# Four of 32 product-key blocks computed from gathered rows instead of dense products, in a two-layer kernel on one core

## The reference

```python
s, i = jax.lax.top_k(sim, k)                       # per head: 8 of 64 keys in either half
all_scores = (sx[..., :, None] + sy[..., None, :]).reshape(b, n, h, k * k)
scores, pk = jax.lax.top_k(all_scores, k)          # 8 of the 64 pairs
idx = jnp.take_along_axis(all_idx, pk, axis=-1)    # 8 heads x 8 = 64 of 4096 rows per token
w_down, w_up = key_in[idx], key_out[idx]
o = jnp.einsum('bnd,bnhkd->bnhk', inputs, w_down)
o = gelu(o) * softmax(scores)
out = jnp.einsum('bnhk,bnhkd->bnd', o, w_up)
```

## Time and profile before

| | |
|---|---|
| median of three runs | 2982.59 us |
| profiled execution, first to last instruction (its span) | 2977.3 us |
| what the three runs have around such a span | about 5.3 us |
| TensorE busy with matmuls | 2840.2 us, 95% of the span |
| VectorE busy | 1919.1 us, 64% |
| ScalarE busy | 1215.2 us, 41% |
| GpSimd busy | 491.4 us, 17% |
| mean granted TensorE clock | 0.985 |
| product-key and LSTM stage, from the first L1008 to the last L1077 | 425.8 to about 1971 us |

### The profile page before, as it was taken

How to read it: one execution, slowest core, us unless ns; L and a number is a source line. 1 busy time by engine, 2 the same in 40 slices (tenths; PEclk the granted TensorE clock), 3 DMA queues, 4 the chain that set the end, 5 groups by cost and what they waited for, 6 DMA issues and landing times.

```text
span 2977.3 us, 72660 instructions
## 1 busy us (share of the span) xinstructions
PE 2840.2 (95%) x28558; PEld 2187.9 (73%) x28558; DVE 1919.1 (64%) x6577; ACT 1215.2 (41%) x2721; POOL 491.4 (17%) x616
## 2 busy tenths in 40 slices
PE   8999979999999999999999999978999859999998
PEld 4895467777777777777777777645676639999998
DVE  4553587777777777777777777466777654444443
ACT  2332232333334343434343333235555525555554
POOL 0555400000000000000000000012334313333333
PEclk9999989999999999999999999999999979999999
DMA  3552300101010000101010101111222232222222
GB/s 141 175 158 82 140 2 23 33 23 34 23 34 30 26 32 25 36 24 34 23 34 23 33 23 33 37 36 41 70 77 63 59 121 33 37 37 40 37 37 33
DMA packets 94322, 148.90 MB, mean 50 GB/s; under 512 B 20048, under 2 KB 76240, under 8 KB 90896
## 3 DMA queue, kind: packets, MB, share of 16 engines
q1 hardware_dynamic: 73728, 107.83, 11.0%
q0 software_dynamic: 20112, 36.40, 6.0%
q10 hardware_dynamic: 144, 0.03, 0.0%
HBM read 95.93 MB, written 48.27 MB: 48 GB/s over the span
## 4 chain that ended last, share of the span: by engine, by line
PE 87%; DVE 6%; DMA 2%; ACT 2%; issue 2%; SPq 0%; POOL 0%; POOLq 0%; DVEq 0%; ACTq 0%
PE ps L1008 16%; PE ps L827 15%; PE ps L2075 9%; PE ps L1077 8%; PE ps L2090 8%; PE ps L1044 4%; PE ps L989 4%; PE ps L420 2%; PE ps L431 2%; PE ps L857 2%; PE ps L858 2%; PE ps L1560 2%; PE ps L1516 1%; PE ps L266 1%; PE ps L267 1%
## 5 line engine op out<-in xcount | busy, mean ns | idle before, releaser
L827 PEld LDWEIGHTS ps<-arena 128*128 128x128 f32 x4096 | 536.4, 192 | 29.1 <-issue 2.9
L1008 PE MATMUL ps<-arena 128*128 128x256 f32 x2048 | 550.7, 392 | 3.0 <-DVE arena L998 2.0
L827 PE MATMUL ps<-arena 128*128 128x128 f32 x4096 | 538.9, 276 | 0.9 <-ACT arena L835 0.9
L1008 PEld LDWEIGHTS ps<-arena 128*128 128x128 f32 x2048 | 354.7, 190 | 164.1 <-issue 132.9
L835 ACT ACTIVATE arena<-ps 128x256 f32<-128x256 f32 x512 | 196.0, 383 | 546.4 <-PE ps L827 545.9
L1077 PE MATMUL ps<-arena 128*16 128x256 f32 x4096 | 270.6, 382 | 8.4 <-DVE arena L1107 7.6
L2075 PE MATMUL ps<-arena 128*128 128x128 f32 x2272 | 265.4, 275 | 0.1
L1803 POOL MEMSET arena<- 128x3072 f32 x1 | 2.7, 2658 | 1569.6 <-PE ps L1008 1569.6
L2075 PEld LDWEIGHTS ps<-arena 128*128 128x128 f32 x2272 | 259.4, 192 | 0.4 <-issue 0.3
L2090 PE MATMUL ps<-arena 128*128 128x256 f32 x1136 | 256.8, 379 | 0.0
L1098 DVE SCALAR_TENSOR_TENSOR arena<-arena 128x128 f32<-128x128 f32 x256 | 73.7, 288 | 280.6 <-ACT arena L1089 280.6
(11 more groups left out here) (287 smaller groups left out, 4631.3 us busy)
## 6 DMA issues: line engine op xcount, KB each, us to landing
xw_scratch<-arena SPq DMA_DIRECT2D x32, 512.0 KB, 2.7
arena<-xw_scratch SPq DMA_DIRECT2D x256, 64.0 KB, 2.7
arena<-in_W SPq DMA_DIRECT2D x16, 1024.0 KB, 5.2
ys_scratch<-arena SPq DMA_DIRECT2D x71, 128.0 KB, 1.8
xn_scratch<-arena SPq DMA_DIRECT2D x32, 129.0 KB, 3.0
arena<-in_xT SPq DMA_DIRECT2D x8, 512.0 KB, 8.1
arena<-in_kinT SPq DMA_DIRECT2D x8, 512.0 KB
arena<-in_xtb SPq DMA_DIRECT2D x32, 128.0 KB, 2.2
```

What stands on the lines that cost most here:

```text
L827: m = e.matmul(bank(b)[:, 128 * i:128 * i + 128], kin[:, k, 2 * jp + i, :], xcT[:, k, 128 * blk:128 * blk + 128], start=(k == 0), stop=(k ...
L1008: m = e.matmul(bank(7)[:, 0:256], G[blk % 2][:, j, :], kout[:, j, :], start=(j == 0), stop=(j == 31))
```

## The change

Four of the 32 blocks (numbers 6, 13, 20 and 27, called sparse) no longer have dense products. The loop over i now runs over the other 28 blocks (`ND`), listed in `DB`. The sparse blocks are worked on beside them. The global slot number is g = 16 i + jp, and sparse block k is laid out around g = C = 16 * (6, 12, 18, 24)[k]:

- slots C-95 to C-65: similarity in four quarters of 256 columns in a free half of a PSUM bank, top keys, softmax and row numbers on VectorE;
- slots C-64 to C-37: 64 gathers by GpSimd, one for each of the 64 chosen rows per token, each of 128 rows of key_in (1 KB a row), into a ring of `NR` = 5 tiles; VectorE takes each with a `tensor_tensor_reduce` of 128 x 256 (2 or 3 in a slot);
- slots C-35 to C-32: gelu, weights, transposes;
- slots C-30 to C-3: 64 gathers of key_out rows into the same ring; TensorE takes each with a matmul of 32 stationary columns (`s_out_tensor`); ScalarE spreads the weights into the stationary tile eight times;
- slots C-3 to C+12: sum, x1, transposes, L1044's product in two halves in a bank of its own.

The gathers of key_out rows are used only ahead of a step, all that are due at once, and the step comes behind them on TensorE. LSTM steps have new places: at least 1.5 slots apart (so 1 and 2 slots in turn), not before `ready` of their block; 244 of the 256 lie in the loop and 12 behind it. With the constants of the diff the turns in which key_out rows are used, and how many, are for each of the four blocks (slot relative to C: number): -30: 2, -29: 2, -27: 4, -22: 11, -20: 5, -19: 2, -17: 4, -16: 3, -14: 4, -13: 2, -11: 5, -6: 11, -4: 4, -3: 5.

New work of TensorE in a shared bank waits (`window`) until VectorE has read the weight group before it, and the weight group behind it (`window_end_tensor`) waits for the readers of that work. The diff, cut to its core:

```diff
+        NR = 5
+        ring = [take(256) for _ in range(NR)]
+        SPARSE_AT = (6, 12, 18, 24)
+        NSP, ND = len(SPARSE_AT), 32 - len(SPARSE_AT)
+        SB = [c + k for k, c in enumerate(SPARSE_AT)]
+        DB = [b for b in range(NBLK) if b not in SB]
-        LAG = 13
-        def step_of(i, k):
-            t = 8 * i - LAG + k
-            return range(t, t + 1) if 0 <= t < 8 * NBLK else ()
+        GAP10 = 15
+        END = 16 * ND
+        def ready(b):
+            return 16 * SPARSE_AT[SB.index(b)] + 17 if b in SB else 16 * DB.index(b) + 26
+        step_pos, turn10 = [], 0
+        for t in range(8 * NBLK):
+            turn10 = max(turn10 + GAP10, 10 * ready(t // 8))
+            if t % 8 == 7 and t // 8 + 1 < NBLK:
+                turn10 = max(turn10, 10 * input_product(t // 8 + 1) + 10)
+            step_pos.append(-(-turn10 // 10))
+        def window(e, k, o):
+            g = 16 * SPARSE_AT[k] + o
+            e.wait_ge(s["A"], 4 * (g // 16) + 4 + g % 16 // 4 + 1)
+        def s_sim_tensor(e, k, q):
+            window(e, k, -93 + 4 * q)
+            e.matmul(low5, x_s[:, 0, :], Kc[:, 0, 256 * q:256 * q + 256], start=True, stop=False)
+            e.matmul(low5, x_s[:, 1, :], Kc[:, 1, 256 * q:256 * q + 256], start=False, stop=True)
+        def s_free_gpsimd(e, u):
+            if u >= 0:
+                k, r = u // 128, u % 128
+                if r < 64:
+                    e.wait_ge(s["s_dot"], 64 * k + r + 1)
+                else:
+                    e.wait_ge(s["s_out"], 64 * k + r - 63)
+        def s_in_gpsimd(e, k, r):
+            j, landed, n = s_slot(128 * k + r)
+            s_free_gpsimd(e, 128 * k + r - NR)
+            row_gather_gpsimd(e, ring[j], kin_rows, iu_s[:, r:r + 1], landed)
+        def s_dot_vector(e, k, r):
+            e.wait_ge(landed, n)
+            e.tensor_tensor_reduce(ring[j], ring[j], x_s.rearrange("p c d -> p (c d)"), 1.0, 0.0, ALU.mult, ALU.add,
+                                   o_s[:, r:r + 1]).then_inc(s["s_dot"], 1)
+        def s_rows_gpsimd(e, k, n):
+            s_free_gpsimd(e, 128 * k + 64 + n - NR)
+            row_gather_gpsimd(e, ring[j], kout_rows, iT_s[:, n:n + 1], landed)
+        def s_out_tensor(e, k, n):
+            g, c = n % 4, n // 8
+            e.wait_ge(s["cb"], CB + 16 * k + 2 * c + 2)
+            e.wait_ge(landed, m)
+            e.matmul(acc[32 * g:32 * g + 32], Dg[c % 2][:, n % 8, :], ring[j], start=False, stop=(n >= 60),
+                     skip_group_check=True).then_inc(s["s_out"], 1)
+        IN_AT, IN_N, OUT_AT, OUT_N = -64, 28, -30, 29
+            turns = [g for g in range(C + OUT_AT, C + OUT_AT + OUT_N) if steps_at[g]]
+            for g in turns:
+                due = 64 if g == turns[-1] else 64 * (g - C - OUT_AT + 1) // OUT_N
 ...
-            for i in range(-2, NBLK):
+            for i in range(-2, ND):
                 for jp in range(16):
-                    if jp % 2 == 0:
-                        for t in step_of(i, jp // 2):
-                            step_tensor(e, t)
+                    for t in steps_at[g]:
+                        for k, n in outs(g):
+                            e.wait_ge(s["seed"], t + 1)
+                            s_out_tensor(e, k, n)
+                        step_tensor(e, t)
 ...
+                    dots = share(g, IN_AT, IN_N)
+                    for k, r in dots[0:1]:
+                        s_dot_vector(e, k, r)
                     for t in steps_at[g]:
                         hidden_vector(e, t)
 ...
+        def peer_gpsimd(e):
+            for k in range(NSP):
+                for r in range(64):
+                    s_in_gpsimd(e, k, r)
+                for n in range(NR):
+                    s_rows_gpsimd(e, k, n)
+                for n in range(NR, 64):
+                    s_rows_gpsimd(e, k, n)
-    nc = bacc.Bacc("TRN2", target_bir_lowering=False, num_devices=1)
+    nc = bacc.Bacc("TRN2", target_bir_lowering=False, num_devices=1, dynamic_dma_scratch_size=8192)
```

More of the change, by code:

```diff
@@ new lines, in s_index_vector, with s_slot @@
+        def s_index_vector(e, k):
+            e.wait_ge(s["s_pe"], 7 * k + 6)
+            e.tensor_copy(by_four(iT_s)[0], halves(low)[0])
+            e.tensor_copy(by_four(iT_s)[1], halves(low)[1]).then_inc(s["s_u7"], 1)
+        RING = [(f"xs{i}", row_count(56 + i)) for i in range(4, 8)] + [("s_r4", 0)]
+        CB, YM = 8, 8
+        def s_slot(u):
+            name, before = RING[u % NR]
+            return u % NR, s[name], before + 16 * (u // NR + 1)
+        def s_free_gpsimd(e, u):
[5 more added lines that the diff above has]
+                    e.wait_ge(s["s_out"], 64 * k + r - 63)
@@ new lines, in s_xw_tensor, with s_xw_vector @@
+        def s_xw_tensor(e, k, h):
+            b = SB[k]
+            window(e, k, 7 + 4 * h)
+            for c in range(2):
+                m = e.matmul(bank(4), xcT[:, c, 128 * b:128 * b + 128], Wx[:, c, 512 * h:512 * h + 512], start=(c == 0),
+                             stop=(c == 1))
+            m.then_inc(s["s_xw"], 1)
+        def s_xw_vector(e, k, h):
+            e.wait_ge(s["s_xw"], 2 * k + h + 1)
+            if h == 0:
+                e.wait_ge(s["xws"], 16 * SB[k])
+            e.tensor_tensor(xWn[:, 512 * h:512 * h + 512], bank(4), lbr[:, 2 * h:2 * h + 2].rearrange("p g f u -> p (g f u)"),
+                            ALU.add).then_inc(s["xWd" if h else "ym"], 1)
@@ new lines, in build @@
+        IN_AT, IN_N, OUT_AT, OUT_N = -64, 28, -30, 29
+        out_of, zero_of, sum_of = {}, {}, {}
+        for k in range(NSP):
+            C, n = 16 * SPARSE_AT[k], 0
+            zero_of[[g for g in range(C + OUT_AT - 5, C) if steps_at[g]][0]] = k
+            turns = [g for g in range(C + OUT_AT, C + OUT_AT + OUT_N) if steps_at[g]]
+            for g in turns:
+                due = 64 if g == turns[-1] else 64 * (g - C - OUT_AT + 1) // OUT_N
+                out_of[g], n = (k, n, due), due
+            sum_of[turns[-1]] = k
@@ L1128, in peer_tensor, with outs @@
+        def outs(g):
+            if g in out_of:
+                k, a, b = out_of[g]
+                return [(k, n) for n in range(a, b)]
+            return []
         def peer_tensor(e):
@@ L1206, in peer_scalar @@
+                    for k in sparse_at(g, -32):
+                        s_weights_scalar(e, k)
+                    for c in range(8):
+                        for k in sparse_at(g, -32 if c < 2 else OUT_AT + 2 - (-OUT_N * (c - 1) // 8)):
+                            s_spread_scalar(e, k, c)
+                    for k in sparse_at(g, 4):
+                        s_x1_scalar(e, k)
                 if i == -2:
@@ new lines, in peer_vector @@
+                    if more and jp == 1:
+                        place2_vector(e, i + 2)
+                    if more and jp == 5:
+                        rows_vector(e, i + 2)
+                    if more and jp == 7:
+                        ztrans_vector(e, i + 2)
+                    if next_ and jp == 8:
+                        best_vector(e, i + 3, 0, 8)
+                    if next_ and jp == 9:
+                        best_vector(e, i + 3, 8, 16)
+                    if next_ and jp == 11:
+                        place_vector(e, i + 3, 2, 4)
@@ new lines, in peer_vector @@
+                    if next_ and jp == 12:
+                        place_vector(e, i + 3, 6, 11)
+                    if next_ and jp == 13:
+                        place_vector(e, i + 3, 11, 16)
+                    for k, r in dots[1:]:
+                        s_dot_vector(e, k, r)
+                    for k in sparse_at(g, -74):
+                        s_pairs_vector(e, k)
+                    for k in sparse_at(g, -73):
+                        s_best2_vector(e, k, 0)
+                    for k in sparse_at(g, -72):
+                        s_best2_vector(e, k, 4)
@@ L1274, in peer_vector @@
+                    if more and jp == 15:
                         onehot_vector(e, i + 2, 0)
-            for k in range(LAG):
-                for t in step_of(NBLK, k):
-                    cell_vector(e, t)
-                    hidden_vector(e, t)
+            for k in range(TAIL):
+                cell_vector(e, IN + k)
+                hidden_vector(e, IN + k)
                 if k == 1:
-                    xw_vector(e, NBLK - 1)
+                    xw_vector(e, ND - 1)
                 for n in norms_of(k):
```

469 lines of the change are left out of this document (353 added, 116 removed).

## The result

The changed kernel takes 3128.58 us (3126.11 to 3130.55, 4 runs) against 2982.24 us for the kernel before: a ratio of 1.0492, 95% interval 1.0477 to 1.0506, or 146 us more. Run again on another occasion it took 3130.89 us, ratio 1.0509 (1.0491 to 1.0526).

What follows compares the result with a forecast made beforehand. TensorE's own queue was taken as the bound. -134.5 + 36 + 14 + 0 + 93 + 30 + 16 = +54.5 on a span of 2977.3, with 5.3 us around it, gave 3037 us; range 2950 to 3120.

Steps and rivals of the forecast that it cites:

- the rows: TensorE waits for gathered key_out rows, mainly in eight turns of eleven rows: +93 us, bounds 47 to 110.
- removed, less the small matmuls: On TensorE, a sparse block loses 33.6 us of work (134.5 for four) and gains 9.0 in small matmuls and transposes (+36).
- steps closer together: One-slot distances between LSTM steps are 0.21 us too short for the step's chain; 68 of them cost +14 us (0 to 40).
- waits for rows, and the clock: TensorE waits for gathered rows, +93 us, and its clock falls after turns of eleven rows, +16 us (0 to 35).
- VectorE: In the windows of dots and top-k VectorE is level with TensorE; they wait on each other, +30 us (0 to 100).
- the test that the prediction set itself: TensorE's waits on gathered rows at the small matmuls: near 90 us in total; the prediction is wrong if under 60.
- the 80 that the text gave as a sign of its being wrong: TensorE's waits on VectorE: 20 to 60 us expected; the prediction is wrong if over 80 us.
- the case of GpSimd as the bound in the dots: Rival: gathers in the dots take 1.91 us each, 122 us against a window of 90; about 3190 us, chance 0.04.
- The rule of the Trainium skill, "SBUF — State Buffer": GpSimd cannot write descriptors while VectorE runs a two-port copy, cast or tensor_scalar; it speaks against gathers beside a busy VectorE.
- (a): Rival: only the gathered rows are late, VectorE and clock cost nothing; +8.5 us, 2991 us, chance 0.12.
- (b): Rival: the change pays, row waits are half (47 us), all waits together under 98 us; 2945 us, chance 0.2.
- (c): Rival: VectorE becomes the bound in the windows of dots and top-k, 100 us instead of 30; 3107 us, chance 0.12.
- The end of the loop: The last two turns get 21 steps instead of 16, with fewer steps elsewhere; together 0 us (-4 to +6).

Runs made afterwards that it cites:

- experiment 1: Changed kernel with no sparse block: 3089.39 us with steps 1.5 slots apart, 2980.28 us with two slots, against 2982.24 us for the kernel before.
- 3: Changed kernel with small matmuls reading a resident tile of key_out, no gathered rows: 3121.87 us, then 3030.39 us (ratio 1.0175) on another chip.
- experiment 4: Changed kernel with dots over 8 of 256 columns, gathers and waits kept: 3092.99 us, ratio 1.0378 against 1.0509 for the changed kernel.
- the dense program: Changed kernel with all 32 blocks dense, no sparse block: 3089.39 us with steps 1.5 slots apart, 3016.91 us with 1.7.
- resident rows and 1.7 slots: Changed kernel with steps 1.7 slots apart and small matmuls reading a resident tile of key_out, without its gathers: 2989.08 us, ratio 1.0032.

## Why the prediction was wrong

The direction was right, and so was the size of the term it called decisive, the rows; the time was not, 3128.58 against 3037 and a range that ended at 3120. In cycles of seven blocks the account nearly closes:

| part, us a cycle | predicted | measured | by |
|---|---|---|---|
| removed, less the small matmuls | -33.6 + 9.0 | not by itself | |
| steps closer together | 14 / 4 = 3.5 | 7 x (52.05 - 48.72) = 23.3 | 1 |
| waits for rows, and the clock | (93 + 16) / 4 = 27.3 | 24.5 | 3 |
| VectorE | 7.5 | 10.5 | 4 |
| sum | 13.7 | 33.7 with the predicted removal | cycle: 34.8 |

**Removed work, small matmuls.** The sum closes to 1.1 us with the predicted -24.6, which fits a removal of that size but doesn't measure it. Part of the fit is luck: the dense program has 21 one-slot distances and seven pauses in seven blocks, the changed kernel 25 and three in a cycle. By the number of distances alone, 25 x 1.18, the steps' line would be 29.5 and the sum 40. At 1.7 slots it does not close, with the 10.5 for VectorE carried over from 1.5: -24.6 + 7 x (49.87 - 48.72) + 3.5 + 10.5 = -2.6, while the cycle is 344.7 - 341.0 = +3.7. Those 6 us a cycle are open. A candidate is that sparse blocks make the close steps dearer: the wait of L1102 is 50 us with resident rows and 1.7 slots, and 34.2 in the dense program. Another is a term that the prediction put at nothing: the small matmuls wait for ScalarE to spread the weights (L1376), 9.0 us in the changed kernel and 11.6 with resident rows and 1.7 slots. Both were seen, not tested.

**Steps closer together: the step that failed.** The prediction priced a one-slot distance as 3.05 - 2.84 = 0.21 us, with the 3.05 from the last turns of the loop. There VectorE ran the step's four instructions and nothing else, 1.02 of the 3.05 us. In the middle of the stage it is busy for 34.66 of 47 us, the chain passes through its queue four times a step, and the distance is 3.4 and 4.0 us in the rows of experiment 1. It was +107 and not +14, and the bound of 40 in the text was too low as well. And the prediction counted distances and never looked at their grouping; the transposes' wait (L964, 26.7 us in the dense program with 1.5 slots, 0.6 with 1.7) is a cost that a count of short distances doesn't have. This term is the miss: with 107 in its place the sum would have been 3130. That this is within 2 us of the measured time is partly luck, for the reason above, and because the prediction added 5.3 us around the span (from two different executions), where the runs on record have 1.8 to 3.1 each.

**Rows for TensorE, and the clock.** Right in mechanism, place and size: 8.3 + 1.5 + 2 = 11.8 us were expected over a slot with its step in a turn of eleven, and the one shown has 11.8; 109 us in all, measured 100. Wrong was the test that the prediction set itself, waits of 90 us on rows and a sign of being wrong under 60: the table shows 40.7, with 2.8 us as the longest, since a matmul at the 1.2 GHz level counts 1.03 us as busy where it counted 0.59. The Trainium skill, "TensorE: Matmul & The Clock Gate", part 1, says that an idle array is put to half rate; the trace agrees in the turn shown (1.00 to 0.50).

**VectorE.** +30 for the windows of dots and top-k was expected, and most of the dots' arithmetic alone measured 38; a dot takes 0.415 us and 0.08 for its accumulator, where up to 0.41 was taken. The wait of TensorE on the hidden state is 74.2 us and the transposes' 19.8, over the 80 that the text gave as a sign of its being wrong, but most of that comes with the steps' distances (61.8 and 26.7 with no dots at all).

**GpSimd.** 1.25 us from gather to gather in the shown turn, as expected; the case of GpSimd as the bound in the dots did not come. Few gathers were slow beside VectorE's work: the median in the stage is 949 ns, for key_out's rows and for those of key_in, which land beside the dots.

```profile
L206 POOL DMA_INDIRECT arena<-in_kout,arena x256: 943/949/1931, 609.1 to 1877.3; - x128
L206 POOL DMA_INDIRECT arena<-in_kinr,arena x224: 943/949/1962, 560.2 to 1730.0; - x112
```

The rule of the Trainium skill, "SBUF — State Buffer", that was weighed against this change doesn't show in the median; the slow gathers, up to 1962 ns, were not followed up.

**The rivals.** (a), rows alone, fell with the 38 us of experiment 4, and (b), all waits under 98 us, with 100 us for rows and clock and 94 us of waits on VectorE. (c) gave nearly the right time, 3107, by luck and by the wrong cause: most of the loss is there with no dots at all, because VectorE's queue is late for close steps. No version tried beats the kernel before; the best complete one, with 1.7 slots, is 1.6% slower.

**Not settled.** The 6 us a cycle at 1.7 slots; whether one exchanged block pays by itself; what exactly is late on the slow-feeding chips, and whether the chip or the occasion decides it. The end of the loop (predicted 0) was not measured alone.

## What to carry to other kernels

When a change takes slots out of a hand-written order, the work that is left has to fit into fewer slots: price the closer spacing of the recurrent chain first, and take its period from a stretch where the other engines carry their full load, never from the emptied end of a loop. Ask not only how many rows a ring holds but how demand is grouped: here pauses in the steps made the turns that emptied the ring, and one spacing constant was worth 102 us, while never asking for more than the ring holds made a good spacing 19 us slower. Where waits consist of short matmuls in a trickle, the table of waits understates them; the distance from slot to slot does not.

## What was not expected of the hardware

The same kernel took 3247.3 us on one chip and 3100.35 on another, and another 3121.87 and 3030.39, while the kernel before was within 0.3% on all of them (2980.22 to 2982.89 us). Four chips were met: two showed it in every kernel with gathers in this stage (22.1 to 88.4 us of matmul idle time ended by "issue" on L1006), two in none (0.9 us at most). Before a small difference is read from one chip, the idle time of TensorE that nothing explains should be compared on it.
